# First tile of a two-attention decoder layer: output-weight rounding moved behind the first scores, rotary gathers split five and three, x(1) loaded earlier, mask loads later

## What is computed

```python
xq = apply_rotary_emb((x @ Wq).reshape(b, s, 32, 16)); xk = apply_rotary_emb((x @ Wk).reshape(b, s, 8, 16))
scores = einsum('bqhd,bkhd->bhqk', xq, repeat(xk, 4)) / sqrt(16)
scores = where(causal, scores, -inf)
out = einsum('bhqk,bkhd->bqhd', softmax(scores), repeat(xv, 4)).reshape(b, s, 512)
x = layernorm(x + out @ Wo)                       # Wo is the weight whose rounding is moved
cos = cos_t[position_ids]; sin = sin_t[position_ids]   # the rotary gathers, for the cross-attention
```

## Time and profile before

| | us |
|---|---|
| median of 3 runs (lowest to highest) | 819.03 (818.23 to 821.03) |
| profiled execution, its own time | 817.94 |
| its span in the trace | 816.0 |
| PE busy | 758.6 (93%) |
| DVE busy | 607.5 (74%) |
| POOL busy | 392.2 (48%) |
| ACT busy | 317.6 (39%) |

### The profile page before, as it was taken

How to read it: one execution, slowest core, us unless ns; L and a number is a source line. 1 busy time by engine, 2 the same in 40 slices (tenths; PEclk the granted TensorE clock), 3 DMA queues, 4 the chain that set the end, 5 groups by cost and what they waited for, 6 DMA issues and landing times.

```text
span 816.0 us, 13861 instructions
## 1 busy us (share of the span) xinstructions
PE 758.6 (93%) x4800; PEld 649.0 (80%) x4800; DVE 607.5 (74%) x1165; ACT 317.6 (39%) x669; POOL 392.2 (48%) x369
## 2 busy tenths in 40 slices
PE   4689999989999999999999999999999999989984
PEld 3577777779878887888888888888888888877763
DVE  4778888877787676676677768677766776788767
ACT  4455555562433323343333334324233333333313
POOL 7566666664545544453544445444444644442102
PEclk9899999999999999999999999999999999999998
DMA  9500004012343232222232222242222232120002
GB/s 264 118 18 17 16 16 119 3 55 53 81 127 79 64 81 79 62 53 51 78 77 77 77 51 51 53 103 75 51 77 51 55 78 75 46 85 1 1 0 103
DMA packets 107875, 53.53 MB, mean 66 GB/s; under 512 B 80449, under 2 KB 96961, under 8 KB 107841
## 3 DMA queue, kind: packets, MB, share of 16 engines
q1 hardware_dynamic: 107008, 51.51, 24.7%
q10 hardware_dynamic: 576, 1.05, 0.4%
q0 software_dynamic: 256, 0.52, 0.2%
HBM read 32.62 MB, written 2.10 MB: 43 GB/s over the span
## 4 chain that ended last, share of the span: by engine, by line
PE 64%; DVE 19%; issue 6%; POOL 4%; ACT 2%; DMA 2%; SPq 2%; DVEq 0%; ACTq 0%; POOLq 0%
PE bank L723 17%; PE bank L658 17%; PE bank L484 10%; DVE arena_r L1512 5%; PE s_bank L737 3%; PE bank L534 2%; PE s_bank L739 2%; PE bank L707 2%; PE bank L558 2%; DVE small L1600 2%; DVE arena_f L1594 1%; PE s_bank L707 1%; ACT arena_r L979 1%; PE s_bank L558 1%; DMA arena_f<-in_L_attn_Wo 1%
## 5 line engine op out<-in xcount | busy, mean ns | idle before, releaser
L723 PE MATMUL bank<-arena_r 128*128 128x512 f32 x768 | 192.2, 399 | 0.9 <-DVE arena_r L1512 0.9
L979 ACT ACTIVATE arena_r<-bank 128x256 fp32r<-128x256 f32 (+2 forms) x249 | 105.1, 458 | 222.6 <-PE bank L690 88.6
L658 PE MATMUL bank<-arena_r 128*128 128x512 f32 x720 | 185.2, 400 | 2.2 <-POOL arena_r L1396 1.6
L723 PEld LDWEIGHTS bank<-arena_r 128*128 128x128 f32 x768 | 139.9, 189 | 28.2 <-DVE arena_r L1512 1.3
L658 PEld LDWEIGHTS bank<-arena_r 128*128 128x128 f32 x720 | 130.7, 188 | 31.5 <-POOL arena_r L1396 2.1
L484 PE MATMUL bank<-arena_r 128*128 128x256 f32 (+1 forms) x1056 | 146.7, 295 | 1.5 <-DVE arena_r L1512 0.6
L484 PEld LDWEIGHTS bank<-arena_r 128*128 128x128 f32 x1056 | 137.4, 191 | 9.0 <-DVE arena_r L1512 1.5
L1512 DVE TENSOR_TENSOR arena_r<-bank,arena_r 128x256 fp32r<-128x256 f32 (+2 forms) x217 | 99.9, 486 | 58.5 <-ACT arena_r L979 57.9
L979 ACT ACTIVATE arena_r<-arena_f 128x512 fp32r<-128x512 f32 (+2 forms) x178 | 104.4, 637 | 61.6 <-DMA arena_f<-arena_f 47.7
L1512 DVE TENSOR_TENSOR arena_r<-arena_f,arena_r 128x512 fp32r<-128x512 f32 (+1 forms) x100 | 92.9, 937 | 17.6 <-ACT arena_r L979 17.5
L1387 POOL TENSOR_TENSOR arena_f<-arena_f 128x512 f32<-128x512 f32 x30 | 39.2, 1306 | 114.2 <-DVE arena_f L1681 114.2
(11 more groups left out here) (153 smaller groups left out, 1169.9 us busy)
## 6 DMA issues: line engine op xcount, KB each, us to landing
arena_f<-arena_f SPq DMA_DIRECT2D x120, 128.0 KB, 2.5
arena_f<-in_L_xattn_Wo SPq DMA_DIRECT2D x8, 1024.0 KB, 5.6
arena_f<-in_L_xattn_Wq SPq DMA_DIRECT2D x14, 512.0 KB, 4.1
arena_f<-in_x SPq DMA_DIRECT2D x8, 256.0 KB, 2.8
arena_f<-in_x SPq DMA_DIRECT2D x1, 2048.0 KB, 15.5
arena_f<-in_L_xattn_Wk SPq DMA_DIRECT2D x8, 256.0 KB, 3.1
arena_f<-in_L_xattn_Wv SPq DMA_DIRECT2D x8, 256.0 KB, 3.3
arena_f<-in_ctx SPq DMA_DIRECT2D x8, 256.0 KB, 3.1
```

Source lines behind the costliest of these rows:

```text
L658: mm = pe.matmul(BQ2[f][:], w2q_s[a][:, e, j, f, :], xT[b][:, e, tok], start=(e == 0 and n == 0), stop=(e == EC - 1 and n == 2))
L723: mm = pe.matmul(BO2[i][:], at2[a][:, h, i * P:(i + 1) * P], w2o_s[b][:, h, :], start=(h == 0 and n == 0), stop=(h == HG - 1 and n == 2))
L979: act.activation(dst, src, ACT.Copy).then_inc(done, 1)
```

## The change

- SP: `next_x(1)` goes ahead of the eight pieces of Wo. The two halves of the mask no longer follow `res`: the first goes behind the values of tile 0 and x(2), the second behind the rotary tables.
- ACT: the four high parts of `w1out`, with the wait for their load, go from ahead of tile 0 to behind its query and key copies, ahead of `expo(0, 0)`.
- DVE: the four low parts of `w1out` leave tile 0. Two stand in tile 1 between `masked_max(1, 0)` and `masked_max(1, 1)`, two behind `total(1, 1)`, ahead of `masked_max(1, 3)`.
- POOL: five gathers stay ahead of the tiles; three go into tile 0 behind the low part of the stacked keys, ahead of `sub(0, 0)`.
- PE: nothing is changed.

```diff
@@ SP
             sp.dma_start(causal[:], c_causal).then_inc(d_const, 16)
+            next_x(1)
             w1o_v = w1o.rearrange("(g h d) n -> g d h n", g=G1, h=HG)
             for g in range(G1):
                 sp.dma_start(w1out_raw[D1 * g:D1 * g + D1, :, :], w1o_v[g]).then_inc(d_w1o, 16)
-            next_x(1)
             sp.dma_start(res, x.rearrange("(t p) n -> p t n", p=P)).then_inc(d_res, 16)
-            for i in range(2):
+
+            def load_mask(i):
                 sp.dma_start(mask_i[S * i:S * i + S, :].rearrange("q (b k) -> q b k", b=B),
                              mask.rearrange("b q k -> q b k")).then_inc(d_mask, 16)
@@ SP
             next_x(2)
+            load_mask(0)
             sp.wait_ge(r_table, 2)
...
+            load_mask(1)
             with sp.Fori(1, T - 2) as t:
@@ ACT
-            act.wait_ge(d_w1o, 16 * G1)
-            for h in range(HG):
-                copy(w1out[0][:, h, :], w1out_raw[:, h, :], s_w1oh)
@@ ACT, tile_steps
                 if old:
                     at_high(v, not oldest)
+                else:
+                    act.wait_ge(d_w1o, 16 * G1)
+                    for h in range(HG):
+                        copy(w1out[0][:, h, :], w1out_raw[:, h, :], s_w1oh)
                 expo(i, 0)
@@ POOL
-            for t in range(T):
+            for t in range(T - 3):
                 gather_rope(t)
@@ POOL, tile_steps, behind the low part of the stacked keys
+                if not old:
+                    for t in range(T - 3, T):
+                        gather_rope(t)
@@ DVE
+            def w1out_low(h):
+                dve.wait_ge(s_w1oh, h + 1)
+                low(w1out[1][:, h, :], w1out_raw[:, h, :], w1out[0][:, h, :], s_w1ol)
@@ DVE, tile_steps
                 rope_k(i, not old)
-                if not old:
-                    for h in range(HG):
-                        dve.wait_ge(s_w1oh, h + 1)
-                        low(w1out[1][:, h, :], w1out_raw[:, h, :], w1out[0][:, h, :], s_w1ol)
...
                 masked_max(i, 0, not old)
                 if oldest:
                     norm1(w)
+                elif old:
+                    w1out_low(0)
+                    w1out_low(1)
                 masked_max(i, 1, not old)
...
                 total(i, 1)
                 if oldest:
                     x1_low(w)
+                elif old:
+                    w1out_low(2)
+                    w1out_low(3)
```

## The result

| | before | changed |
|---|---|---|
| median of 6 runs (lowest to highest), us | 819.22 (818.23 to 821.03) | 826.46 (824.06 to 828.43) |
| profiled execution, its own time | 817.94 | 828.43 |
| its span | 816.0 | 825.5 |

The ratio is 1.0083, 95% interval 1.0064 to 1.0102: 7.2 us slower. The forecast was 823.3 (4.3 slower), with a range up to 826.5; the result lies at the very edge of it, and nearest to rival C (825.9). The profiled execution of the changed kernel is the slowest of its six, which matters for the last 2.3 us of the account.

The account below looks back on a forecast made before the run. The prediction took the wait chain's first 60 us as deciding, DVE pacing from mid tile 0 through most of tile 1, then TensorE. 5.9 + 1.9 - 3.5 = 4.3 us slower gave 823.3, range 820.0 to 826.5.

Parts of the forecast that it names:

- rival C: Everything contends: gathers land at 27.9, L is 1.2, TensorE loses a whole product's 2.3 us; 6.9 slower, 825.9; chance 0.15.
- Tile 1, the low parts of Wo: TensorE's first output projection in tile 1 waits for DVE's four low parts, starting 5.9 us later.
- 54.28 + 4L: Time in us at which the four low parts of Wo end in tile 1, forecast as 57.9.
- L: Duration of one low part of Wo on DVE, taken as 0.91 us; bounds 0.69 and 1.67.
- Clock in tile 1: TensorE, 5.1 us idle in tile 1, falls to 1.2 GHz; the work behind loses 1.9 us (0 to 4.6).
- Tile 0, the queries: Stacked queries' transposes start 4.45 us earlier and run 1.26 us faster, so the first mask comes 5.7 us earlier.
- The three gathers: In tile 0 `table_turn` waits for the last gather, landing at 26.9; of 5.7 us gained 3.5 remain.
- What passes on: The 3.5 us left at tile 0's third mask pass on, as DVE has no idle time until mid tile 1.
- Mask loads, x(1), Wo: The moved loads: nobody waits for them, taken as zero; ACT's high parts of Wo cost at most 0.3 us.
- Rival A: The clock stays high in tile 1, all else as forecast: 2.4 us slower, 821.4; chance 0.17.
- Rival B: Gathers land in time, tile 0's full 5.7 us reach tile 1: 818.4, or 820.3 with a clock fall; chance 0.13.
- G: Landing time of the last gather in tile 0, taken as 26.9 us; the wait decides once over 24.7.

Follow-up runs that it names:

- experiment 1: Changed kernel with the rounding of Wo back in its old places on ACT and DVE, loads and gathers kept changed: 820.09 us, ratio 1.0024.
- experiment 3: Kernel before with only the rounding of Wo moved on ACT and DVE, nothing of SP or POOL: 825.02 us, ratio 1.0084.
- experiment 4: Changed kernel with the four low parts of Wo in tile 0 behind the first total instead of in tile 1: 817.79 us, ratio 0.9998.
- experiment 5: Changed kernel with the second pair of low parts ahead of tile 1's first total instead of behind its second: 822.97 us, ratio 1.0056.
- experiment 10: Kernel of experiment 9 with table transposes behind tile 0's second scores and ACT's table copies behind the second exponential: 815.46 us, ratio 0.9970.
- experiment 8: Changed kernel with 18 overwritten matmuls in TensorE's wait ahead of the first output projection: 824.30 us, ratio 1.0058.
- experiment 6: Changed kernel with 24 overwritten matmuls in TensorE's wait ahead of the first output projection: 826.93 us, ratio 1.0108.
- experiment 7: Changed kernel with 14 overwritten matmuls in TensorE's wait ahead of the first output projection: 825.52 us, ratio 1.0096.
- experiment 2: Changed kernel with all eight gathers ahead of POOL's first sum: 825.81 us, ratio 1.0088.
- experiment 11: Kernel of experiment 10 with ACT's two table copies behind the copy of the values instead of ahead of it: 815.49 us, ratio 0.9973.
- experiment 9: Changed kernel with Wo's rounding in tile 0: high parts behind ACT's values copy, low parts behind DVE's low part of the stacked queries: 816.64 us, ratio 0.9986.

## Why the prediction was right, and where its sizes were off

The way, the wait and the path were right; the size was too small by 2.9 us, and what makes the clock fall was read wrongly. The measured 826.46 is nearer to rival C's 825.9, which had a chance of 0.15, than to the forecast. Point by point, in the prediction's terms:

- *Tile 1, the low parts of Wo* (5.9 us): right in kind and shown by experiments 1, 3, 4 and 5. Counted from where tile 1 stood in the changed kernel (1.8 us early), the output projection started 57.13 - (52.02 - 1.80) = 6.9 us late. The sum 54.28 + 4L holds; L was 1.16 (2.05 us for the first pair, 2.57 for the second, from the starts) and not 0.91. POOL's subtractions and multiplications stand beside most of them; in experiment 10, with POOL mostly at its gathers, the four took 3.02 us, 0.75 each.
- *Clock in tile 1* (1.9 us): a term of its own, 2.5 us; experiment 8 shows it. The whole product ran at the low clock, so the price of a whole product, 2.3 to 2.5, was the better value. Two readings behind this term do not hold. The 5.29 us of the earlier trace rows, called a product at the low clock, stand in a stretch where the profile shows the high one (rows below; the changed kernel's took 4.58 us in the same place, at 1.00 too). Products at a shown 0.50 took 5.45 to 5.49 us, so it was luck that 5.29 was near. And the length of the wait did not draw the fall: the clock fell at 52.2, only 0.9 us behind the last score at 51.30. Ahead of that stood an idle time of 1.42 us that the kernel before doesn't have, because the first pair of low parts delays the second mask, and 1.1 us of scores. In experiments 6 and 8 the clock fell at 52.3 and 54.0 although the added matmuls were already running; in 7, with the same order up to there, it fell only at 57.5. What decides between these is not shown.
- *Tile 0, the queries* (5.7 us at the first mask): 5.07 measured. The 4.45 at the transposes were 4.96, as the query projection ended about 0.7 us earlier in this execution. But the 4.51 us from transposes to first mask, which assumed 2.4 GHz, were 5.66: the clock fell behind 3.17 us of idle time. That choice was wrong.
- *The three gathers*: right that `table_turn` waits, and for 2.75 us. The last was issued at 21.54 and took 4.5 us, so it landed at 26.0; 4.6 had been taken, with an issue at 22.3. The way from there to the third mask was 4.0 us and not 2.3, since TensorE's clock fell again in that wait: eight table transposes took 2.0 us instead of 1.06, the scores 1.9 instead of 1.1.
- *What passes on* (3.5 us): 2.6 at the third mask, and then only 1.85 at tile 1's rotary product. "The 3.5 pass on" failed as a step: the query projection of tile 1, at the low clock for 5.47 us, became the bound there. The prediction named this fall in rival C and left it out of the sum. From 3.5 to 1.85 this is the largest error, 1.7 us: half of it was lost by the third mask, half at the query projection.
- *Mask loads, x(1), Wo* (nothing): right. The two mask issues took 0.65 and 1.18 us and held nobody; nobody waited for x(1); ACT's first exponential started on POOL's subtraction.

```profile
8.00:9.00 1.00, 1.00 (x3) 0.81 (x4) 0.88 (x2) 0.58 (x1) 0.70 (x2) 1.00 1.15 167
10.00:11.00 1.00, 1.00 (x4) 0.71 (x3) 0.00 (x0) 0.16 (x1) 0.94 (x1) 1.00 1.09 207
```

These two rows are stretches of the kernel before, with its granted clock behind POOL's busy time, for the point on the clock.

Together 6.9 + 2.5 - 1.8 = 7.6 us at tile 2, against a measured 7.2 in the medians. The estimate worked out from the Trainium skill ("DMA: Bandwidth & Descriptors", section "Anatomy of one DMA — SWDGE (gpsimd) path"), 2.2 us behind the issue, would have had the gather land at 24.7; it landed at 26.0, 3.5 us behind the issue's end.

Rival A (the clock stays high) did not come: all four traces in which TensorE waited through without added work (this one and experiments 2, 3 and 5) show the fall. Rival B failed at its own condition: G was 26.0, over 24.7. Rival C's terms came in part: L near its 1.2, a whole product's 2.3, and the fall in tile 0; only the gathers were not as late as it took them.

What stays open: why the two best kernels, 10 and 11, don't differ in the medians although one profiled execution of each does. Both traces show one more fall of the clock, for 3.4 us from 163 and 161 us, behind which some 1.2 us of the lead are gone. Neither has the low spell of the kernel before at 733 us, where they win 1.0 and 1.4 us back. Whether the other executions have it can't be told. And why experiment 1 is 0.24% over the kernel before is only read from its trace (the gathers' wait), not tried apart.

## What to carry to other kernels

Before a step is moved, look up every wait for its result, in every engine's order, and not only the engine that runs it: the moved work cost DVE little, and its consumer on TensorE, one tile on, 7 us. (SP waits for the same low parts, L442, ahead of loads that it issues at 135.5 us; that wait cost nothing.) Put such work where the trace shows its engine idle ahead of the first consumer's wait; in the same kernel that place left no cost that the runs can tell (experiment 9). And price an idle time that you open on TensorE at its length plus what the work behind it loses at 1.2 GHz, here 2.5 us for twelve matmuls, and do not count on a short one being free.

## What the runs showed that I had not expected

- The clock fell behind short idle times: behind 1.42 us of idle and 0.9 us of 64-column score matmuls (experiment 5), and 0.3 us into the work behind an idle time of 3.17 us (tile 0 of the changed kernel). It also fell under running matmuls (experiments 6 and 8).
- The low clock outlasts the idle time: in the changed kernel it held over 5.3 us of the work behind the wait of tile 1, and from about 25 to 35 us in tile 0.
- The last three gathers took 4.5, 4.4 and 4.5 us from issue to landing, the first five 6.2 to 8.3 in the same execution.
